# A six-layer perceiver block on one core: when the second batch's values are projected, which PSUM banks hold the last group's turned scores, and how the result is combined and stored

## The chip, the cores and the metric

The kernel runs on one core of one Trainium2 chip. Its engines, as the profile names them, are PE (TensorE, matrix products; PEld is its loading of weights), DVE (VectorE), ACT (ScalarE), POOL (GpSimd) and SP (SyncE, which only issues DMAs here). They have a program each and wait for one another through semaphores. The metric is the device time of one execution in microseconds (us), lower is better. Timed before the change: 976.12 us, the median of three runs (973.57 to 976.53).

## The reference, cut to what matters

Two batches of 256 tokens, 256 channels, pass through six residual layers: cross-attention over a context of 4096 rows per batch (16 heads of 16 channels), a gated convolution block, a quantised feed-forward layer, a second cross-attention, a self-attention, and a mixture of eight experts. The change touches the first and the last.

```
def _L0_xattn_ref(q, k, v, mask, ...):        # first layer, 16 heads, 4096 keys per batch
    q = (layernorm(x) @ Wq.T + bq), k = (ctx @ Wk.T + bk), v = (ctx @ Wv.T + bv)   # by heads of 16
    out = softmax(q @ k.T / 4, masked) @ v
    return out @ Wo.T + bo
...
def _L1_ffn_ref(x, expert_embeddings, first_linear, second_linear):   # last layer
    tokens = x_flat[index].reshape(E, expert_capacity, hidden)        # 64 tokens for each of 8 experts
    inter = jax.nn.relu(jnp.einsum('ech,eih->eci', tokens, first_linear))
    out = jnp.einsum('eci,ehi->ech', inter, second_linear) * vals[:, :, None]
    final = jnp.zeros((n_tokens, hidden), x.dtype).at[index].add(out.reshape(-1, hidden))
x = x + final
```

## The kernel before, in words

**The first cross-attention** takes more than half of the time. A *group* is four heads of one batch; there are eight (numbered 0 to 7 by `gg`, 0 to 3 belong to the first batch). In a group the 4096 keys are taken in 32 *steps* of 128, and the loops go by *pairs* of steps, `m` from 0 to 15. In the order of the PE program, one pair is (with the lines of the profile):

- T, the turned scores (`turned_scores`, L1815): for each step four bf16 matmuls of 256 columns, two to a PSUM bank, so two banks a step. ACT takes the exponential of each bank (`exps`, L756, 128x512), two instructions a step. Below, "exp" is one such instruction.
- S, the row scores of the *next* group (`scores`, L1786): two matmuls of 512 columns, one unit after each step. DVE takes their maximum (`row_tops`, L1119). They run ahead, so that they are all done before the last pairs of group 6; group 7 has none.
- K, a projection of second-batch keys (`project_keys`, L1753), in every second pair of groups 0 and 1.
- C, in pair 1 of a group, the turning of the finished context of the group before (`turn_context`, L1843).
- W, the weighing of values by the exps of the pair *before* (`weigh_values`, L1833): 4 fp32 matmuls of 32 weight columns a step.
- V, a projection of second-batch values (`project_values`, L1763, four fp32 matmuls of 256 columns into one bank), 16 of them, in pairs 1 to 15 of group 3 and pair 0 of group 4. ACT copies the bank to SBUF (`copy_values`, L739).

In the last pair of a group stand also the tops of the next (`turn_max`, L1800, copied by ACT at L747).

The eight PSUM banks are divided so: 0 to 3 hold the row scores S, two units of two banks. Banks 4 to 6 are a ring of three (`RING`) for T, K, V, C and tops, in one order that the function `ring_slots` counts out. `ring_free(slot)` lets PE write slot n only when ACT has drained slot n-3. Bank 7 collects W. PE and ACT both go strictly in their program's order. ACT's order in a pair is: four exps, key copies, in pair 1 the context's copy, in pair 0 the copy of the finished weighing of the group before (`copy_weighed`, L763), then the value copy. In pair 8 of group 7 a small matmul (L1885) sums up the absolute weights of the feed-forward layer, on which the DVE's quantising (L1174 to L1190) and then three weight loads wait.

**The last layer** ends with `combine(q)` (L2473): for each pair q of experts, for each tile i of 128 tokens, one matmul that adds into the PSUM bank i. DVE adds bank i to the residual tile (L1738) once `g_out` says that its q = 3 is done, and SP stores all four tiles with one DMA of 512 KB (L629), when all are added.

Of the kernel before, what the change touches and what calls it, by code (L numbers as in the profile page):

```python
# [11 lines left out]
ALU = mybir.AluOpType  # L12
# [3 lines left out]
P = 128  # L16
# [72 lines left out]


def ring_slots():

    turn = itertools.count()
    keys, values, exps, tops, contexts = {}, {}, {}, {}, {}
    for c in range(ROUNDS):
        for i in range(2):
            if c < NCH:
                keys[0, c, i] = next(turn)
            if c in VALUES_AT:
                values[0, VALUES_AT[c], i] = next(turn)  # L100
    for pair in range(2):
        tops[0, pair] = next(turn)
    for gg in range(GROUPS):
        for m in range(KC // 2):
            if m == KC // 2 - 1 and gg + 1 < GROUPS:
                for pair in range(2):
                    tops[gg + 1, pair] = next(turn)
            for step in (KC * gg + 2 * m, KC * gg + 2 * m + 1):
                for pair in range(2):
                    exps[step, pair] = next(turn)  # L110
            if gg < 2 and m % 2:
                keys[1, 4 * gg + m // 4, m // 2 % 2] = next(turn)
            if gg and m == 1:
                contexts[gg - 1] = next(turn)
            if (gg == 3 and m) or (gg == 4 and m == 0):
                done = KC // 2 * (gg - 3) + m - 1
                values[1, done // 2, done % 2] = next(turn)
    contexts[GROUPS - 1] = next(turn)
    return keys, values, exps, tops, contexts
# [3 lines left out]


def values_after(gg, m):

    if (gg == 3 and m) or (gg == 4 and m == 0):
        return divmod(KC // 2 * (gg - 3) + m - 1, 2)
    return None

# [8 lines left out]
def build(nc, t):  # L139

    ctx = ExitStack()
    with ctx:
# [63 lines left out]
        def ring_heads(slot):  # L206
            return ring_bank(slot).rearrange("p (j n) -> p j n", j=2)

        def unit_banks(n):
# [237 lines left out]
        def _(sp):  # L447
# [179 lines left out]
            load(EMB, by_part("embT"), "const_loaded")  # L627
            sp.wait_ge(on["x_ready"], 6 * TT)
            sp.dma_start(t["out"].rearrange("(t p) c -> p t c", p=P), X).then_inc(out_stored, 16)  # L629
            sp.wait_ge(out_stored, 16)  # L630

# [73 lines left out]
        def _(act):  # L705
# [44 lines left out]
            def exps(step):  # L750
                for pair in range(2):
                    slot = EXP_AT[step, pair]
                    act.wait_ge(ring_filled, slot + 1)
                    if pair == 0 and step >= 4:
                        act.wait_ge(pv_done, step - 3)
                    nc.scalar.activation(PR[step % 4][:, pair * CH:(pair + 1) * CH], ring_bank(slot), ACT.Exp)\  # L756
                      .then_inc(ring_drained, 1)
# [298 lines left out]
        def _(dve):  # L1056
# [113 lines left out]
            def quantise_weights():  # L1170
# [7 lines left out]
                dve.wait_ge(on["w_total"], 1)  # L1178
                mark(nc.vector.tensor_scalar(WMEAN, psum[:, 0, 0:2], 1.0 / (D * FF), 1e-5, ALU.mult, ALU.max))
                done()  # L1180
# [561 lines left out]
        def _(pe):  # L1742
# [61 lines left out]
            def turned_scores(step, masked):  # L1804
# [5 lines left out]
                for pair in range(2):  # L1810
                    slot = EXP_AT[step, pair]
                    ring_free(slot)
                    for u in range(2):
                        j = 2 * pair + u
                        last = nc.tensor.matmul(ring_heads(slot)[:, u, :], KST[gg % 2][0:KROWS, j, kc * P:(kc + 1) * P],  # L1815
                                                QST[0:KROWS, G * g + j, b * S:(b + 1) * S],
                                                start=(u == 0), stop=not masked and u == 1, skip_group_check=True)
                    if masked:
                        for qt in range(2):
                            last = nc.tensor.matmul(ring_heads(slot)[:, :, qt * P:(qt + 1) * P],  # L1820
                                                    MASKB[:, qt, kc * P:(kc + 1) * P],
# [25 lines left out]
            def attend(masked):  # L1847
# [17 lines left out]
                for gg in range(GROUPS):  # L1865
                    for m in range(KC // 2):
# [8 lines left out]
                        if gg and m == 1:  # L1875
                            turn_context(gg - 1)
                        if gg or m:
                            weigh_values(KC * gg + 2 * m - 2)
                            weigh_values(KC * gg + 2 * m - 1)
                        if values_after(gg, m):  # L1880
                            project_values(1, *values_after(gg, m))
                        if gg + 1 == GROUPS and m == KC // 4:
                            pe.wait_ge(on["w_summed"], 2)
                            pe.wait_ge(s_maxed, GROUPS * UNITS)
                            nc.tensor.matmul(psum[:, 0, 0:2], ONES, WSUM, start=True, stop=True)\  # L1885
                              .then_inc(on["w_total"], 1)
# [582 lines left out]

            def combine(q):  # L2470
                pe.wait_ge(on["g_down_copied"], q + 1)
                for i in range(TT):
                    last = nc.tensor.matmul(psum[:, i, 0:256], SELT[:, q, i * P:(i + 1) * P], OE[:, q, :],  # L2473
# [24 lines left out]
            pe.wait_ge(on["g_turned_copied"], 4)  # L2498
            for q in range(4):
                combine(q)  # L2500

# [65 lines left out]
```

## Time and profile before

| | |
|---|---|
| median of three runs | 976.12 us |
| the profiled execution: its own time, its span | 976.69 us, 974.6 us |
| PE, DVE, ACT, POOL busy | 92%, 62%, 49%, 11% of the span |
| TensorE clock granted, mean | 0.968 of full speed |
| groups 0 to 7 of the first cross-attention | about 112 to 539 us of the span |
| in them: second-batch values (V) | 285.7 to 362.8 us |
| in them: group 7 | 499.1 to 539.3 us |
| combine and store | 963.6 us to the end |

The span runs from the first to the last instruction; the execution's own time is 2.1 us longer. "Chain of waits" below is the chain of work that ended last, followed back from the end: each of its pieces released the next. The number behind x counts PE instructions as the hardware has them: an fp32 matmul of the program shows as two.

### The profile page before, as it was taken

To read this page: it belongs to the slowest core of one execution; us is meant where nothing else is said; L and a number is where in the kernel's file an instruction comes from. 1 tells how busy PE (TensorE), PEld (TensorE's weight loads), DVE (VectorE), ACT (ScalarE), POOL (GpSimd) and SP (SyncE) were. 2 spreads that over 40 slices of the span, in tenths; PEclk is the share of its full clock that TensorE was granted. 3 is DMA by queue.
4 is the path that set the end of the run, shared out by engine and by line. 5 is a ranking of instruction groups with operands and counts; after the bars stand their busy time and mean duration, and the time that the engine had idled before them with its cause. 6 is when DMAs were issued, how large, how long until landed. Compare 5 with 4: busy or idle time off the path is not lost.

```text
span 974.6 us, 15294 instructions
## 1 busy us (share of the span) xinstructions
PE 896.3 (92%) x5988; PEld 529.3 (54%) x5988; DVE 608.5 (62%) x1083; ACT 479.8 (49%) x953; POOL 105.7 (11%) x118
## 2 busy tenths in 40 slices
PE   6888999999999999999998898689899999989878
PEld 3445544444555555545544686444784874555635
DVE  5778688778874548888833586847424227379442
ACT  3331557777765557777788432324321210576211
POOL 3320011111000000000000200101000006245100
PEclk9999999999999999999999999869899999999979
DMA  9775634354222011222432600604545640000000
GB/s 312 259 202 199 204 104 141 114 162 138 86 67 76 33 59 56 74 74 74 168 123 79 242 1 1 239 21 152 194 173 208 224 145 29 1 1 1 1 1 22
DMA packets 68836, 108.68 MB, mean 112 GB/s; under 512 B 7062, under 2 KB 42902, under 8 KB 66838
## 3 DMA queue, kind: packets, MB, share of 16 engines
q1 hardware_dynamic: 67100, 101.40, 31.5%
q10 hardware_dynamic: 1664, 6.29, 1.8%
q8 instruction: 49, 0.80, 0.3%
q14 instruction: 23, 0.19, 0.1%
HBM read 93.77 MB, written 13.89 MB: 110 GB/s over the span
## 4 chain that ended last, share of the span: by engine, by line
PE 78%; DVE 6%; ACT 6%; issue 3%; DMA 3%; SPq 2%; POOL 0%; ACTq 0%; DVEq 0%
PE psum L1833 13%; PE psum L1815 11%; PE psum L1786 9%; PE psum L2207 6%; PE psum L2180 5%; PE psum L1969 5%; PE psum L1763 4%; PE psum L2300 4%; PE psum L1753 4%; PE psum L1982 3%; ACT arena L756 3%; DMA kparts<-arena 2%; PE psum L2354 2%; PE psum L2339 1%; PE psum L2372 1%
## 5 line engine op out<-in xcount | busy, mean ns | idle before, releaser
L1119 DVE TENSOR_REDUCE arena<-psum 128x1 f32<-128x1024 f32 x256 | 301.3, 1218 | 109.9 <-PE psum L1786 109.4
L756 ACT ACTIVATE arena<-psum 128x512 f32<-128x512 f32 x512 | 264.6, 603 | 62.1 <-PE psum L1815 61.0
L1815 PE MATMUL psum<-arena 99*128 99x256 bf16 x1024 | 160.2, 274 | 8.9 <-ACT arena L756 4.8
L1786 PE MATMUL psum<-arena 96*128 96x512 bf16 x512 | 152.9, 381 | 8.9 <-DVE arena L1119 4.0
L1815 PEld LDWEIGHTS psum<-arena 99*128 99x128 bf16 x1024 | 79.4, 97 | 107.1 <-ACT arena L756 50.3
L1833 PE MATMUL psum<-arena 128*32 128x256 f32 x2048 | 136.8, 385 | 0.0
L1833 PEld LDWEIGHTS psum<-arena 128*32 128x32 f32 x2048 | 53.5, 109 | 75.4 <-ACT arena L756 36.9
L1753 PE MATMUL psum<-arena 128*128 128x512 f32 x128 | 62.9, 619 | 8.4 <-DMA arena<-ctxT 8.4
L1763 PE MATMUL psum<-arena 128*128 128x256 f32 x256 | 64.7, 389 | 2.1 <-issue 2.1
L1786 PEld LDWEIGHTS psum<-arena 96*128 96x128 bf16 x512 | 49.0, 98 | 28.5 <-DVE arena L1119 11.9
L649 POOL TENSOR_TENSOR arena<-arena 128x512 bf16<-128x512 f32 x34 | 41.4, 1218 | 194.3 <-DVE arena L1105 191.7
L2207 PE MATMUL psum<-arena 128*128 128x256 f32 x256 | 60.0, 390 | 0.0
L1763 PEld LDWEIGHTS psum<-arena 128*128 128x128 f32 x256 | 47.7, 191 | 18.0 <-issue 9.9
L739 ACT ACTIVATE arena<-psum 128x512 f32<-128x512 f32 x32 | 19.1, 597 | 76.4 <-PE psum L1763 76.4
L2180 PE MATMUL psum<-arena 128*128 128x512 f32 x128 | 56.0, 593 | 0.0
L2207 PEld LDWEIGHTS psum<-arena 128*128 128x128 f32 x256 | 49.2, 197 | 6.6
L1969 PE MATMUL psum<-arena 128*128 128x256 f32 x192 | 47.0, 404 | 3.5 <-ACT arena L818 0.9
L1969 PEld LDWEIGHTS psum<-arena 128*128 128x128 f32 x192 | 38.2, 202 | 11.1 <-ACT arena L926 1.3
L733 ACT ACTIVATE arena<-psum,arena 128x512 bf16<-128x512 f32 x32 | 22.0, 687 | 44.2 <-PE psum L1753 40.3
L2300 PE MATMUL psum<-arena 128*128 128x512 f32 x96 | 41.9, 594 | 0.7 <-ACT arena L919 0.7
L1982 PE MATMUL psum<-arena 128*128 128x256 f32 (+1 forms) x160 | 38.1, 399 | 4.2 <-ACT arena L914 2.2
L1753 PEld LDWEIGHTS psum<-arena 128*128 128x128 f32 x128 | 24.5, 200 | 31.5 <-issue 21.4
(244 smaller groups left out, 959.1 us busy)
## 6 DMA issues: line engine op xcount, KB each, us to landing
arena<-kparts SPq DMA_DIRECT2D x192, 128.0 KB, 2.9
kparts<-arena SPq DMA_DIRECT2D x32, 384.0 KB, 3.6
arena<-ctxT SPq DMA_DIRECT2D x20, 512.0 KB, 4.9
arena<-ctx SPq DMA_DIRECT2D x2, 4096.0 KB, 15.1
arena<-mask SPq DMA_DIRECT2D x8, 1024.0 KB, 5.3
arena<-mask ACTq DMA_DIRECT2D x4, 1024.0 KB, 14.5
arena<-ctxT SPq DMA_DIRECT2D x1, 4096.0 KB, 13.9
arena<-ctxT SPq DMA_DIRECT2D x4, 1024.0 KB, 8.2
```

What stands on the lines that cost most here:

```text
L756: nc.scalar.activation(PR[step % 4][:, pair * CH:(pair + 1) * CH], ring_bank(slot), ACT.Exp)\
L1119: nc.vector.tensor_reduce(MX[g % 2][:, col:col + 1], unit_banks(n).rearrange("p b n -> p (b n)"), AX.X, ALU.max).then_inc(s_maxed, 1)
L1753: last = nc.tensor.matmul(ring_bank(slot), WK[:, k, f * P:(f + 1) * P], CTX[n % SLOTS][:, k, :], start=(k == 0), stop=(k == CT - 1))
L1763: last = nc.tensor.matmul(ring_bank(slot)[:, v * 256:(v + 1) * 256], CTX[n % SLOTS][:, k, (2 * i + v) * P:(2 * i + v + 1) * P], WV[:, k, : ...
L1786: last = nc.tensor.matmul(out, q, KST[g % 2][0:ROWS, j, at], start=True, stop=not masked, skip_group_check=True)
L1815: last = nc.tensor.matmul(ring_heads(slot)[:, u, :], KST[gg % 2][0:KROWS, j, kc * P:(kc + 1) * P], QST[0:KROWS, G * g + j, b * S:(b + 1) * S],
L1833: last = nc.tensor.matmul(PV[32 * j:32 * (j + 1), :], V_flat[:, at:at + 32], PR[step % 4][:, j * S:(j + 1) * S], start=(kc == 0), stop=(kc ...
L1969: last = nc.tensor.matmul(out, weights[:, k, m * P:m * P + width], xs[k], start=(k == 0), stop=(k == n - 1))
L1982: last = nc.tensor.matmul(out, lhs[k], weights[:, k, :], start=(k == 0 and not biased), stop=(k == n - 1), skip_group_check=biased)
L2180: last = nc.tensor.matmul(psum[:, unit % 3, :], QC[:, c, w * P:(w + 1) * P], CTXT[w // 2][:, c, n * 512:(n + 1) * 512], start=(c == 0), st ...
L2207: last = nc.tensor.matmul(psum[:, 6, 0:256], PT1[:, k * P:(k + 1) * P], CTXK[w // 2][:, k, :], start=(k == 0), stop=(k == KC - 1), skip_gr ...
L2300: last = nc.tensor.matmul(psum[:, bank, :], HTF[:, c, i * P:(i + 1) * P], WQKV[which][:, c, half * HALF:(half + 1) * HALF], start=(c == 0) ...
```

## The change

1. `values_after` moves the 16 value projections one pair later: pairs 2 to 15 of group 3 and pairs 0 and 1 of group 4. On PE they now stand in front of W of the same pair, not behind it. The order on ACT keeps its form, and the ring is counted out anew.
2. From step `LAST` (the first of group 7) on, the turned scores go to banks 0 to 3 (`exp_bank`: bank 2 (step mod 2) + pair of heads), which S no longer needs. Each then waits for the exp of two steps before on its own bank; it was the exp three slots of the ring before. The sum of the weights goes into a ring bank (`SUM_BANK`) in place of bank 0.
3. `combine` goes by tile: tiles 0 and 1 get q = 0, 1, 2, then both get q = 3, then tiles 2 and 3 get all four each. The store is four DMAs of 128 KB, each issued once its tile is added.

```diff
+def values_after(gg, m):
+
+    if (gg == 3 and m >= 2) or (gg == 4 and m < 2):
+        return divmod(KC // 2 * (gg - 3) + m - 2, 2)
+    return None
...
-    if (gg == 3 and m) or (gg == 4 and m == 0):
-        return divmod(KC // 2 * (gg - 3) + m - 1, 2)
-    return None
+LAST = (GROUPS - 1) * KC
+SUM_BANK = next(4 + i for i in range(RING) if i not in (CONTEXT_AT[GROUPS - 2] % RING, CONTEXT_AT[GROUPS - 1] % RING))
...
+        def exp_bank(step, pair):
+
+            return psum[:, 2 * (step % 2) + pair, :] if step >= LAST else ring_bank(EXP_AT[step, pair])
...
-            sp.wait_ge(on["x_ready"], 6 * TT)
-            sp.dma_start(t["out"].rearrange("(t p) c -> p t c", p=P), X).then_inc(out_stored, 16)
-            sp.wait_ge(out_stored, 16)
+            for i in range(TT):
+                sp.wait_ge(on["x_ready"], 5 * TT + i + 1)
+                sp.dma_start(t["out"][i * P:(i + 1) * P, :], X[:, i, :]).then_inc(out_stored, 16)
+            sp.wait_ge(out_stored, 16 * TT)
...
                 for pair in range(2):
-                    slot = EXP_AT[step, pair]
-                    ring_free(slot)
+                    heads = exp_bank(step, pair).rearrange("p (j n) -> p j n", j=2)
+                    if step < LAST:
+                        ring_free(EXP_AT[step, pair])
+                    elif step < LAST + 2:
+                        pe.wait_ge(s_maxed, GROUPS * UNITS)
+                    else:
+                        pe.wait_ge(ring_drained, EXP_AT[step - 2, pair] + 1)
...
+                        if values_after(gg, m):
+                            project_values(1, *values_after(gg, m))
                         if gg or m:
                             weigh_values(KC * gg + 2 * m - 2)
                             weigh_values(KC * gg + 2 * m - 1)
-                        if values_after(gg, m):
-                            project_values(1, *values_after(gg, m))
                         if gg + 1 == GROUPS and m == KC // 4:
                             pe.wait_ge(on["w_summed"], 2)
-                            pe.wait_ge(s_maxed, GROUPS * UNITS)
-                            nc.tensor.matmul(psum[:, 0, 0:2], ONES, WSUM, start=True, stop=True)\
+                            nc.tensor.matmul(psum[:, SUM_BANK, 0:2], ONES, WSUM, start=True, stop=True)\
...
-            def combine(q):
-                pe.wait_ge(on["g_down_copied"], q + 1)
-                for i in range(TT):
+            def combine(i, *pairs):
+                for q in pairs:
+                    pe.wait_ge(on["g_down_copied"], q + 1)
...
-            for q in range(4):
-                combine(q)
+            combine(0, 0, 1, 2)
+            combine(1, 0, 1, 2)
+            combine(0, 3)
+            combine(1, 3)
+            combine(2, 0, 1, 2, 3)
+            combine(3, 0, 1, 2, 3)
```

PE's program in pairs 1 to 3 of group 3, before (the copy of the program without mask). L1815 is T, L1786 S, L1843 C, L1833 W, L1763 V:

```order
344 L1843 MATMUL psum<-arena 128x128 x2
345 L1833 MATMUL psum<-arena 32x256 x8
346 L1763 MATMUL psum<-arena 128x256 x4
347 L1815 MATMUL psum<-arena 128x256 x4
348 L1786 MATMUL psum<-arena 128x512 x2
349 L1815 MATMUL psum<-arena 128x256 x4
350 L1786 MATMUL psum<-arena 128x512 x2
351 L1833 MATMUL psum<-arena 32x256 x8
352 L1763 MATMUL psum<-arena 128x256 x4
353 L1815 MATMUL psum<-arena 128x256 x4
```

The same place on PE after the change (L1827 is T, L1793 S, L1855 C, L1845 W, L1770 V):

```order
344 L1855 MATMUL psum<-arena 128x128 x2
345 L1845 MATMUL psum<-arena 32x256 x8
346 L1827 MATMUL psum<-arena 128x256 x4
347 L1793 MATMUL psum<-arena 128x512 x2
348 L1827 MATMUL psum<-arena 128x256 x4
349 L1793 MATMUL psum<-arena 128x512 x2
350 L1770 MATMUL psum<-arena 128x256 x4
351 L1845 MATMUL psum<-arena 32x256 x8
352 L1827 MATMUL psum<-arena 128x256 x4
```

V stood between W and the next T; it now stands between S and W. Pair 1 of group 3 has none. In group 7 and in the combine no kind of instruction changes its place on PE; only banks, waits and the operands of the 16 combine matmuls do.

## Rows read from the trace of the kernel before

**Rows 1.** The page, the chain that ended last, shares by engine.

```profile
PE 78%; DVE 6%; ACT 6%; issue 3%; DMA 3%; SPq 2%; POOL 0%; ACTq 0%; DVEq 0%
```

**Rows 2.** Chain of waits, one pair of group 7: start us, us, what.

```profile
508.32 1.00 PE psum L1833 x16
509.32 0.34 PE psum L1815 x2
...
509.68 0.61 ACT arena L756
...
510.33 0.39 PE psum L1815 x2
```

**Rows 3.** Chain of waits, one pair with values, group 3.

```profile
290.67 1.94 PE psum L1763 x8
...
293.12 0.60 ACT arena L756
...
295.60 1.94 PE psum L1763 x8
```

**Rows 4.** Chain of waits, one pair with a key projection, group 1.

```profile
199.66 1.72 PE psum L1753 x4
201.38 1.00 PE psum L1833 x16
202.38 0.54 PE psum L1815 x4
202.92 0.43 PE psum L1786 x2
203.36 0.44 PE psum L1815 x4
```

**Rows 5.** Chain of waits, a value projection near the start.

```profile
29.68 1.73 PE psum L1763 x8
```

**Rows 6.** Chain of waits, group 2's end to pair 1 of group 4.

```profile
274.99 1.00 PE psum L1833 x16
...
278.82 1.00 PE psum L1833 x16
...
284.52 0.22 PE psum L1843 x2
...
285.74 1.94 PE psum L1763 x8
...
365.02 1.00 PE psum L1833 x16
```

**Rows 7.** Timeline of ACT, runs of 128x512 activations.

```profile
509.68 2.06 ACT L756 ACTIVATE arena<-psum 128x512 f32<-128x512 f32 x4 [0.34 <-PE psum L1815]
...
832.57 4.03 ACT L994 ACTIVATE arena<-psum 128x512 f32<-128x512 f32 x8 [23.82 <-PE psum L2311]
```

**Rows 8.** Chain of waits, turning of the context, pair 1 of group 7.

```profile
503.07 0.44 PE psum L1843 x2
```

**Rows 9.** Chain of waits, the last piece.

```profile
970.82 0.42 DVE arena L1738
```

**Rows 10.** Timeline: the last weight load, its first user, the store's issue.

```profile
530.69 1.55 SPq L561 DMA_DIRECT2D arena<-wfuT  x1
...
549.08 1.29 PE L2098 MATMUL psum<-arena 128*32 128x256 f32 x20
...
971.26 0.38 SPq L629 DMA_DIRECT2D out<-arena  x1
```

**Rows 11.** DMA issues: count, KB each, median us from issue to landing.

```profile
arena<-wfuT SPq DMA_DIRECT2D x1, 1024.0 KB, 7.5
...
out<-arena SPq DMA_DIRECT2D x1, 512.0 KB, 2.9
...
arena<-woT SPq DMA_DIRECT2D x1, 256.0 KB, 2.6
```

**Rows 12.** Windows: PE, PEld, DVE, ACT, POOL busy, granted clock, DMA share, GB/s.

```profile
544.00:545.00 1.00, 1.00 (x3) 0.82 (x4) 0.00 (x0) 1.00 (x1) 1.00 (x4) 0.50 1.03 434
```

More of the change, by code:

```diff
@@ L114, in ring_slots @@
                 contexts[gg - 1] = next(turn)
-            if (gg == 3 and m) or (gg == 4 and m == 0):
-                done = KC // 2 * (gg - 3) + m - 1
-                values[1, done // 2, done % 2] = next(turn)
+            if values_after(gg, m):
+                values[(1, *values_after(gg, m))] = next(turn)
     contexts[GROUPS - 1] = next(turn)
@@ L122 @@
 KEY_AT, VALUE_AT, EXP_AT, TOP_AT, CONTEXT_AT = ring_slots()
-def values_after(gg, m):
-    if (gg == 3 and m) or (gg == 4 and m == 0):
-        return divmod(KC // 2 * (gg - 3) + m - 1, 2)
-    return None
+LAST = (GROUPS - 1) * KC
+SUM_BANK = next(4 + i for i in range(RING) if i not in (CONTEXT_AT[GROUPS - 2] % RING, CONTEXT_AT[GROUPS - 1] % RING))
 def keys_at(gg, m):
@@ L755, in exps @@
                         act.wait_ge(pv_done, step - 3)
-                    nc.scalar.activation(PR[step % 4][:, pair * CH:(pair + 1) * CH], ring_bank(slot), ACT.Exp)\
+                    nc.scalar.activation(PR[step % 4][:, pair * CH:(pair + 1) * CH], exp_bank(step, pair), ACT.Exp)\
                       .then_inc(ring_drained, 1)
@@ L1178, in quantise_weights @@
                 dve.wait_ge(on["w_total"], 1)
-                mark(nc.vector.tensor_scalar(WMEAN, psum[:, 0, 0:2], 1.0 / (D * FF), 1e-5, ALU.mult, ALU.max))
+                mark(nc.vector.tensor_scalar(WMEAN, psum[:, SUM_BANK, 0:2], 1.0 / (D * FF), 1e-5, ALU.mult, ALU.max))
                 done()
@@ L1810, in turned_scores @@
                 for pair in range(2):
-                    slot = EXP_AT[step, pair]
-                    ring_free(slot)
+                    heads = exp_bank(step, pair).rearrange("p (j n) -> p j n", j=2)
[5 more added lines that the diff above has]
+                        pe.wait_ge(ring_drained, EXP_AT[step - 2, pair] + 1)
                     for u in range(2):
                         j = 2 * pair + u
-                        last = nc.tensor.matmul(ring_heads(slot)[:, u, :], KST[gg % 2][0:KROWS, j, kc * P:(kc + 1) * P],
+                        last = nc.tensor.matmul(heads[:, u, :], KST[gg % 2][0:KROWS, j, kc * P:(kc + 1) * P],
                                                 QST[0:KROWS, G * g + j, b * S:(b + 1) * S],
@@ L1819, in turned_scores @@
                         for qt in range(2):
-                            last = nc.tensor.matmul(ring_heads(slot)[:, :, qt * P:(qt + 1) * P],
+                            last = nc.tensor.matmul(heads[:, :, qt * P:(qt + 1) * P],
                                                     MASKB[:, qt, kc * P:(kc + 1) * P],
@@ L1876, in attend @@
                             turn_context(gg - 1)
+                        if values_after(gg, m):
+                            project_values(1, *values_after(gg, m))
                         if gg or m:
```

## The prediction

> **What bounds the kernel now.** I read the shares of the chain of waits first, then the chain in order of time at the three places that the change touches, then ACT's timeline there, and the list of DMA issues for the end. PE holds 78% of the chain [rows 1], so time is won where PE waits or where one of its instructions costs more than it must. Where nothing is in the way, a pair of steps is PE's work alone: W 1.00, T 0.54, S 0.43, T 0.44, S 0.43, in all 2.84 us [rows 4]. The first T after W costs 0.54 and the second 0.44: 0.10 us goes for the change from the 32-column weights of W to full ones.
>
> In the pairs with values the chain leaves PE. V ends at 292.61 (290.67 + 1.94), and the next V starts at 295.60 after a W of 1.00, so 1.99 us lie between V and W [rows 3], where T, S, T, S right behind V would take 1.74 (the 1.84 of the row above less the change of 0.10). The reader is to see the exp at 293.12 in the chain: ACT copies V first, only then begins its four exps, and the last T of the pair needs the first exp drained. That is a wait of 0.25 us in each such pair. V itself takes 1.94 us there, but 1.73 near the start, where it does not follow W [rows 5].
>
> In group 7 there is no S between the T's. The chain goes W 1.00, T 0.34, exp 0.61, T 0.39, with 0.07 of signals: 2.41 us [rows 2]. Of these 1.41 lie between two W's. The fourth bank of a pair is the ring's first again, so the fourth T waits for an exp that could only start after the first T. ACT is not full: its four exps fill 2.06 us and then it waits 0.34 [rows 7].
>
> **The values, pairs of groups 3 and 4.** The move takes no instruction away. V goes between S and W. The row that stands nearest to this is the key projection K, which has that place already: 1.72 us, four instructions of 0.43, nothing extra in front of it, then W at its usual 1.00 and T at its usual 0.54 [rows 4]. So I take V at 1.73 and not at 1.94, and no wait behind it: ACT has the 1.00 of W to copy the bank (0.60), before T comes. Its own bank is free in time: V's slot needs the second exp of its pair; that starts about 0.85 us after the pair's first T and ends by 1.5, while V comes at 1.84. The pair is 1.00 + 1.84 + 1.73 = 4.57 against 4.93.
>
> I count from the end of W in pair 1 of group 3 (285.74, where the first V starts) to the end of W in pair 1 of group 4 (366.02): 80.28 us [rows 6], with 16 V in both versions. New: 16 × 2.84 = 45.5, 16 × 1.73 = 27.7, the tops in the last pair 0.98 (3.83 from W to W where no V is in the pair, less 2.85), the context's turning 0.22 [rows 6], together 74.4. One hitch is new: in pair 0 of group 4 the copy of the finished weighing stands ahead of V's copy on ACT, and waits for W, which now ends after V. V's copy comes some 0.3 us after W, so the T's behind it wait, and the next V a little: 0.4 by estimate, from copies of 0.4 and 0.6. Sum 74.8, gain 5.4 us. The ends: if V costs 1.94 wherever it stands, 16 × 0.21 = 3.4 less, so 2.0. Nothing below that but for new waits (last rival). Behind V in the queues: SP's two loads of context chunks wait for value copies that come a pair later; they have about 60 us before their values are projected, and the loads of stacked keys behind them wait for W anyway.
>
> **Group 7, four banks.** Each T now waits for the exp two steps before. PE alone then needs 0.54 + 0.44 = 0.98 between two W's in place of 1.41 [rows 2, 4], a pair of 1.98. Can ACT follow? Eight activations of this shape in a row take 4.03 us, (4.03 - 0.60) / 7 = 0.49 from start to start [rows 7]; four are 1.96, just under 1.98. The last exp of a pair ends at about 0.36 + 3 × 0.49 + 0.60 = 2.43 after the pair's first T began, and the T on its bank comes at 1.98 + 0.66 = 2.64. So PE sets the pace. That gives 0.43 in each of pairs 2 to 15, 14 × 0.43 = 6.0. Pairs 0 and 1 gain only about 0.1 together: C stands in a ring bank still, needs an exp of the same pair drained, and that hangs on ACT, which does the copy of the weighing between; C began at 503.07 [rows 8] and would begin near 502.9. Together 6.1. The final double W meets its exps just in time (2.43 against 2.48). The sum of the weights moves to a bank that has been free since the start of the group, so costs the same.
>
> The ends of this term: if ACT needs the whole 2.06 for each four, with no overlap from one pair to the next, 14 × (2.41 - 2.06) = 4.9. If the wait stays as it is, 0.
>
> The Trainium skill, "ScalarE: Activation LUTs", section "What ACT_TABLE_LOAD costs", gives an activation with immediate operands 186 ns + 0.833 ns a column, with 93 ns of overlap back to back. By that page an exp of 512 columns is 613 ns and 520 from start to start, and four are 2.08 us: ACT would be the bound, and the term would be 14 × 0.33 = 4.6. The trace disagrees by 0.03 us an instruction, and the row with eight in a row decides for me; the rival below has its own number from the row of four.
>
> What follows group 7 comes earlier as a whole. Its last weight load could be late in place of PE: wfuT was issued at 530.69 and takes 7.5 us to land, so about 538.2, and the product that needs it starts at 549.08 [rows 10, 11]. The load hangs on the sum in pair 8, which itself comes 7 × 0.43 = 3 us earlier, while its user comes 6.1 earlier. The slack of 11 us shrinks to 8. Cost nothing.
>
> **Combine and store.** The 16 matmuls stay 16, and the last tile is finished when it was. The last add still starts about 970.82 [rows 9]: it had waited behind three others on DVE, each 0.44, but the last matmul ends just before it too. What is left is the store, 2.9 us for 512 KB [rows 11], issued at 971.26 [rows 10]. The last one carries 128 KB and has no other behind or beside it; tile 2's is some 1.7 us older. The nearest row has 256 KB in 2.6, 0.3 less for half; for a quarter I go on by the same slope to about 2.4, and as that row had two other loads behind it, a bit lower: gain 0.6. The ends: 0, and three quarters of 2.9, 2.2.
>
> **Sum.** 5.4 + 6.1 + 0.6 = 12.1. The profiled execution took 976.69, so 964.6 on its scale. That execution was 0.57 above the median of the runs shown; on the median's scale it is 964.0. I say 964.2.
>
> One thing moves without being touched: stretches at the low clock (1.2 GHz, half speed). PE ran at 0.50 in 544:545 [rows 12], after some tenths of idle time around 543.5, and there are such stretches near 630 to 648, 684 to 691 and 926 to 938. Their length can differ when all comes 12 us earlier; one that is 3 us longer or shorter is 1.5 us of time. This is in the ranges.
>
> **The rivals.**
> (a) ACT becomes the pace of group 7, at 2.06 or a little more for each four exps. For it: 1.96 and 1.98 are nearly equal. Against it: the run of eight. 14 × 0.08 = 1.1 us less gain: 965.3.
> (b) V costs 1.94 in its new place too, because the 0.21 is its own and not W's. For it: all 13 V's of full pairs in group 3 show 1.94. Against it: the 1.73 of rows 5, and K. 3.4 us less: 967.6.
> (c) The change does not do what it says in group 7: the fourth T still waits, because what holds it is not its bank. Against: the chain names the exp, and the pair is exactly the sum of W, T, exp, T. 6.1 less: 970.3.
> (d) Slower than before. V in front of W holds W up: V must find its bank drained by the second exp of its pair. If ACT ran late in these pairs, PE would stand before V, and all of W behind it, where before W came first and covered that. It decides from 0.35 us of lateness (1.84 - 1.5); to come out 3 us above 976.1 the 15 us between must be lost in 16 pairs, 0.94 us each, so ACT would have to be 1.3 us late. ACT has 4 × 0.49 + 0.49 = 2.45 us of work in a pair of 4.57, and before K, with the same need, PE never stood [rows 4]. Time 979 at that lateness.
>
> **How the numbers follow.** Forecast 0.62, its own range 962.2 to 966.5; (a) 0.13, (b) 0.15, (c) 0.06, (d) 0.02; 0.02 for something unseen near no change. The low end is 961.3: the store at its best 1.6 more, and a shorter cold stretch 1.3 more. The high end 968.8 holds (a) and (b), with a cold stretch a little longer, and leaves (c) and (d) out. Faster by over 0.3% (2.9 us, about what a measurement tells from no change): 0.95, as (c) with a gain of 6 is faster too; within 0.3% 0.03; slower 0.02.
>
> **What would show it.** In group 3 V is followed by W and the start of one V to the next is 4.57 us, V 1.73 in the chain, and no exp in it. If V is 1.94, (b). In group 7, W to W is 1.98 and the chain stays on PE; if exps of ACT follow one another in the chain there and W to W is 2.04 or more, (a); if W to W is 2.41, (c). The last store lands in about 2.3 us. I am wrong as a whole if group 3 or 7 is as long as before, or if the gain there is given back behind 540 us, by a load not landed or by more work at half clock.

## The result, and the profile after

The changed kernel takes 965.93 us, the median of four runs (964.62 to 966.81), against 975.52 us for the kernel before beside it (973.57 to 976.53). The ratio is 0.9903 [0.9882, 0.9924]: 9.6 us less. The profiled execution took 966.37 us, with a span of 964.5, 10.1 less than before. The mean granted clock is 0.968 in both.

The shares of the chain, answering to [rows 1]:

```profile
PE 79%; DVE 6%; ACT 5%; DMA 4%; issue 3%; SPq 2%; POOL 0%; ACTq 0%; DVEq 0%
```

The chain of waits in a pair of group 3 with values, answering to [rows 3] (start us, us, what; `...` stands for rows left out; L1770 is V, L1845 W, L1827 T, L1793 S):

```profile
292.26 1.73 PE psum L1770 x8
293.99 1.00 PE psum L1845 x16
294.99 0.54 PE psum L1827 x4
...
296.84 1.73 PE psum L1770 x8
```

V starts every 4.58 us where it was 4.93. V is down from 1.94 to 1.73, and no exp is left between V and the T's.

The same chain in pair 0 of group 4, where the copy of the finished weighing (L770, ahead of V's on ACT) waits for W, and in pair 1, where the context is turned (L1855):

```profile
354.48 1.00 PE psum L1845 x16
355.48 0.34 PE psum L1827 x2
...
355.83 0.25 ACT arena L746
...
356.30 0.61 ACT arena L763
...
357.79 0.22 PE psum L1855 x2
...
358.03 1.96 PE psum L1770 x8
360.00 1.00 PE psum L1845 x16
```

W to W is 5.52 us here. L746, the copy of V's bank, is in the chain: this is the hitch that the prediction had named. The V behind the context's turning takes 1.96, not 1.73.

The chain in group 7, from the W of pair 1 on, answering to [rows 2] (the turning of the context before it, at 503.07 in [rows 8], starts at 497.87 here):

```profile
498.31 1.00 PE psum L1845 x16
499.31 0.98 PE psum L1827 x8
500.29 0.77 PE psum L1845 x9
```

W to W is 1.98 and the four T's stand as one piece of 0.98, where two pieces of T had an exp between them. ACT's and PE's timelines there, answering to [rows 7] (what stands in brackets is the idle time before and what ended it):

```profile
499.67 28.03 ACT L763 ACTIVATE arena<-psum 128x512 f32<-128x512 f32 x56 [0.60 <-PE psum L1827]
```

```profile
526.19 2.21 PE L1845 MATMUL psum<-arena 128*32 128x256 f32 x32
```

ACT runs 56 exps in one row, (28.03 - 0.60) / 55 = 0.499 us from start to start. That includes some 0.24 us in which the first T of pair 9 stood behind the sum of the weights (its exp starts at 513.76, 1.24 after the one two before it, where 0.97 to 1.01 is usual); without them it is just under 0.495, a quarter of the pair's 1.98. From the W of pair 1 up to that sum the chain is PE alone, behind it the chain runs along ACT's exps. The last double W takes 2.21, where the same row took 1.93 before: its last eight instructions start at 527.76, 0.05 after the end of the last exp.

Behind group 7 PE falls to the low clock level, and again later. Windows of after (length in us, then PE, PEld, DVE, ACT, POOL busy, granted clock, DMA share, GB/s), beside [rows 12]:

```profile
531.00:538.00 7.00, 6.31 (x20) 4.83 (x19) 0.67 (x2) 2.48 (x3) 3.21 (x11) 0.51 1.00 421
545.00:548.00 3.00, 3.00 (x7) 2.44 (x8) 2.09 (x7) 0.70 (x2) 0.00 (x0) 0.50 0.04 14
616.00:643.00 27.00, 18.39 (x67) 12.73 (x68) 15.35 (x44) 6.53 (x11) 0.00 (x0) 0.51 0.36 132
```

0.50 is 1.2 GHz. Before, there was one such stretch here, from 543.5 to 546.9; now there are two, from 531.2 to 538.0 and from 544.8 to 548.2. The same piece of work in the chains of before and of after shows what the second one costs:

```profile
554.50 20.99 PE psum L1969 x96
```

```profile
545.00 22.57 PE psum L1980 x96
```

The end, answering to [rows 9, 11], the last add and the stores (count, KB each, median us from issue to landing):

```profile
961.99 0.42 DVE arena L1745
```

```profile
out<-arena SPq DMA_DIRECT2D x4, 128.0 KB, 1.7
```

Where the 10.1 us of span came from: the stretch of values (end of W in pair 1 of group 3 to the same in group 4, 285.84 to 361.00) is 75.16 instead of 80.28, 5.1 less. Group 7 (494.13 to 528.44) is 34.31 instead of 40.18, 5.9 less. From the last add's end to the end of the span it is 2.1 instead of 3.4, 1.3 less. Together 12.3. The lead over before is 10.9 us at the end of group 7 (528.44 against 539.34): 11.0 from the two places, less 0.1 because the first began 0.1 later. At the start of the last add it is 8.8 (961.99 against 970.82). So 2.1 us were given back between.

### The profile page after: what moved, and what is told of

It reads as the page before. It is cut to its first block, busy times and chain, and to the rows that moved or that the text cites. A ratio compares the mean times of both kernels' runs of the same rounds, so it can differ in the third digit from the quotient of the medians.

```text
span 964.5 us, 15296 instructions
## 1 busy us (share of the span) xinstructions
PE 889.4 (92%) x5988; PEld 530.3 (55%) x5988; DVE 608.8 (63%) x1083; ACT 480.1 (50%) x953; POOL 105.6 (11%) x118
## 4 chain that ended last, share of the span: by engine, by line
PE 79%; DVE 6%; ACT 5%; DMA 4%; issue 3%; SPq 2%; POOL 0%; ACTq 0%; DVEq 0%
PE psum L1845 12%; PE psum L1827 11%; PE psum L1793 10%; PE psum L2218 6%; PE psum L2191 6%; PE psum L1980 5%; PE psum L2311 4%; PE psum L1770 4%; PE psum L1760 4%; PE psum L1993 3%; ACT arena L763 2%; DMA kparts<-arena 2%; PE psum L2365 2%; PE psum L2350 1%; PE psum L2383 1%
## 5 line engine op out<-in xcount | busy, mean ns | idle before, releaser
L1793 PE MATMUL psum<-arena 96*128 96x512 bf16 x512 | 152.9, 381 | 11.0 <-DMA arena<-kparts 5.9
L1827 PE MATMUL psum<-arena 99*128 99x256 bf16 x1024 | 155.1, 274 | 3.5 <-ACT arena L754 1.2
L1845 PE MATMUL psum<-arena 128*32 128x256 f32 x2048 | 137.0, 385 | 0.1
L1827 PEld LDWEIGHTS psum<-arena 99*128 99x128 bf16 x1024 | 80.6, 97 | 98.2 <-ACT arena L763 36.7
L1845 PEld LDWEIGHTS psum<-arena 128*32 128x32 f32 x2048 | 53.4, 109 | 74.6 <-ACT arena L763 31.1
L1793 PEld LDWEIGHTS psum<-arena 96*128 96x128 bf16 x512 | 48.8, 98 | 30.6 <-DVE arena L1126 13.0
L1770 PE MATMUL psum<-arena 128*128 128x256 f32 x256 | 63.2, 383 | 2.1 <-issue 2.0
L1770 PEld LDWEIGHTS psum<-arena 128*128 128x128 f32 x256 | 48.1, 192 | 15.0 <-issue 6.9
L1980 PE MATMUL psum<-arena 128*128 128x256 f32 x192 | 48.6, 413 | 3.5 <-ACT arena L825 0.9
L746 ACT ACTIVATE arena<-psum 128x512 f32<-128x512 f32 x32 | 19.1, 598 | 58.0 <-PE psum L1770 58.0
L1980 PEld LDWEIGHTS psum<-arena 128*128 128x128 f32 x192 | 39.3, 208 | 11.6 <-ACT arena L933 1.3
L740 ACT ACTIVATE arena<-psum,arena 128x512 bf16<-128x512 f32 x32 | 22.0, 687 | 43.5 <-PE psum L1760 39.4
L1993 PE MATMUL psum<-arena 128*128 128x256 f32 (+1 forms) x160 | 38.5, 401 | 4.2 <-ACT arena L921 2.2
```

Of the source, the lines that this page charges most:

```text
L1770: last = nc.tensor.matmul(ring_bank(slot)[:, v * 256:(v + 1) * 256], CTX[n % SLOTS][:, k, (2 * i + v) * P:(2 * i + v + 1) * P], WV[:, k, : ...
L1793: last = nc.tensor.matmul(out, q, KST[g % 2][0:ROWS, j, at], start=True, stop=not masked, skip_group_check=True)
L1827: last = nc.tensor.matmul(heads[:, u, :], KST[gg % 2][0:KROWS, j, kc * P:(kc + 1) * P], QST[0:KROWS, G * g + j, b * S:(b + 1) * S], start= ...
L1845: last = nc.tensor.matmul(PV[32 * j:32 * (j + 1), :], V_flat[:, at:at + 32], PR[step % 4][:, j * S:(j + 1) * S], start=(kc == 0), stop=(kc ...
L1980: last = nc.tensor.matmul(out, weights[:, k, m * P:m * P + width], xs[k], start=(k == 0), stop=(k == n - 1))
L1993: last = nc.tensor.matmul(out, lhs[k], weights[:, k, :], start=(k == 0 and not biased), stop=(k == n - 1), skip_group_check=biased)
```

## The experiments

Each is built on one of the two kernels. Kernels measured in one session share the runs of before, so the time of before differs a little from case to case (976.8 to 977.2).

**Values alone.** Part 1 of the change on the kernel before (the new `values_after` with it):

```diff
...
+                        if values_after(gg, m):
+                            project_values(1, *values_after(gg, m))
                         if gg or m:
                             weigh_values(KC * gg + 2 * m - 2)
                             weigh_values(KC * gg + 2 * m - 1)
-                        if values_after(gg, m):
-                            project_values(1, *values_after(gg, m))
```

> Part 1 alone: values one pair later and in front of the weighing. Theory: V 1.73 us in its new place, from one V to the next 4.57, groups 3 and 4 shorter by 5.1 us as in the changed kernel; time 975.5 - 5.1 = 970.4, give or take 1.5 for low-clock stretches. Rival (the gain needs the other parts, or V costs 1.94 when alone): 973.5.

972.42 us (8 runs) against 977.02, ratio 0.9946 [0.9924, 0.9968]: 5.3 us less by the ratio, 4.6 by the medians. The median is 0.5 above the range that I expected. The place itself is as expected: V at 1.73, V to V 4.58, and the stretch of values is 75.16 us (287.69 to 362.85), as in the changed kernel. Behind group 7 this execution has a long stretch at the low clock, which comes up again below.

**Late, but still behind W.** The same slots one pair later, V left in its old place:

```diff
-    if (gg == 3 and m) or (gg == 4 and m == 0):
-        return divmod(KC // 2 * (gg - 3) + m - 1, 2)
+    if (gg == 3 and m >= 2) or (gg == 4 and m < 2):
+        return divmod(KC // 2 * (gg - 3) + m - 2, 2)
```

> Values one pair later, but still behind the weighing (half of part 1). Theory: it is the place and not the lateness that counts, so V still 1.94 us, the wait of 0.25 still there, 4.93 from V to V, and 975.5, no change. Rival: the lateness alone gives part of the 5.1, time 971 to 974.

976.76 us (12 runs) against 977.02, ratio 0.9979 [0.9958, 1.0000]. The chain:

```profile
292.47 1.94 PE psum L1764 x8
...
294.44 0.02 ACT arena L740
...
294.93 0.60 ACT arena L757
...
296.40 1.00 PE psum L1834 x16
297.40 1.94 PE psum L1764 x8
```

V is 1.94, V to V is 4.93 and the exp is in the chain, all as before. From the end of W in pair 1 of group 3 to the end of W in pair 2 of group 4 it is 83.13 us (284.70 to 367.83), a plain pair of 2.85 more than the 80.28 of before. The gain hangs on the place in front of W. The delay of a pair gives nothing in the chain; for the whole kernel the interval reaches from no change to 4.1 us less.

**Keys behind the weighing.** The converse, on the changed kernel: K goes to the place that V had (the ring and ACT's order follow, which the diff leaves out).

```diff
-                        if keys_at(gg, m):
-                            project_keys(1, *keys_at(gg, m))
                         if gg and m == 1:
                             turn_context(gg - 1)
...
                             weigh_values(KC * gg + 2 * m - 1)
+                        if keys_at(gg, m):
+                            project_keys(1, *keys_at(gg, m))
```

> The changed kernel with the 16 key projections of groups 0 and 1 moved from in front of the weighing to behind it (the place that values had before). Theory (an fp32 product with 128 weight columns costs 0.21 us more right behind the 32-column weighing, and ACT's copy then stands before the exps): K 1.93 us in place of 1.72, a wait of 0.2 to 0.3 (more, as ACT makes two copies of 0.6), from one K to the next (two pairs) 7.9 to 8.4 in place of 7.41; 8 to 15 us more in all, about 977. Rival (the 0.21 was the value projection's own): K stays 1.72.

983.09 us in one execution, span 981.3, 16.7 more than the changed kernel's profiled one. K to K (two pairs):

```profile
195.83 1.93 PE psum L1760 x4
...
197.78 0.03 ACT arena L740
...
198.37 0.68 ACT arena L741
199.05 0.50 ACT arena L763
...
203.26 1.00 PE psum L1845 x16
204.26 1.93 PE psum L1760 x4
```

K rises from 1.72 to 1.93, by the same 0.21 as V, though it is other work. So the 0.21 belongs to the place behind W and not to V. The rows of PEld show where it sits, here V behind W in before, behind S in after, and behind the turning of the context in after:

```profile
290.60 1.59 PEld L1763 LDWEIGHTS psum<-arena 128*128 128x128 f32 x8 [0.41 <-issue]
```

```profile
287.40 1.61 PEld L1770 LDWEIGHTS psum<-arena 128*128 128x128 f32 x8 [0.21 <-issue]
```

```profile
358.00 1.59 PEld L1770 LDWEIGHTS psum<-arena 128*128 128x128 f32 x8 [0.23 <-issue]
```

By the chain these three V's begin at 290.67, 287.69 and 358.03. A load of these weights takes 0.19. Behind S the first one starts 0.29 before V and is done when V begins; behind W it starts 0.07 before and behind the context's turning 0.03 before, and V is 0.21 and 0.23 longer. The weights of the turning are 128 columns wide like V's own. So the change from 32 columns to 128 can't be the whole reason for a late first load. Behind W it may be; behind the turning, whose two products take 0.22 in all, V's bank is also freed by the third exp of the pair, which ends at 357.89. No run separates these.

The period is 8.43 instead of twice 2.84 plus 1.73, 7.41. The wait is larger than V's: ACT makes two copies of K (L740, L741) before its first exp. Period and time came out above what I had expected, the time by 6 us.

**Four banks alone.** Part 2 on the kernel before (`exp_bank`, `LAST` and `SUM_BANK` as in the change's diff, the values and the end as before).

> Part 2 alone: group 7 in four banks. Theory: 1.98 us from W to W in group 7, 5.9 us less up to the end of the last W. After it the changed kernel ran 6.9 us at the low clock where before had 3.5. If that comes from how group 7 now runs, this kernel shows the long stretch right behind the last W too, and 971.0 to 971.5; if it is only where the stretch falls, 969.6 give or take 1.5.

971.14 us (6 runs), ratio 0.9938 [0.9915, 0.9962]: 6.1 us less by the ratio, 5.9 by the medians. The chain, W to W 1.98:

```profile
504.33 0.98 PE psum L1826 x8
505.31 1.00 PE psum L1844 x16
```

It has the long stretch at the low clock behind group 7 (534.0 to 540.8), and the time is the one that I had expected with it. The conclusion that I had tied to this, that the stretch comes from how group 7 runs, does not hold: see the part on why the prediction was right.

**Combine and store alone.** Part 3 on the kernel before.

> Part 3 alone: combine by tile, four stores. Theory: from the last add to the end 2.1 us in place of 3.4, all else as before: 974.2. Rival (the stores cost issue time or the order of the combine matmuls costs PE time): 975.5 or more.

976.37 us (12 runs), ratio 0.9999 [0.9985, 1.0014]. Its last add ends at 971.57 and the span at 973.7, so the end is 2.1 us as it is after the change, while the total can't show 1.3; the 974.2 that I expected did not come. The interval reaches from 1.5 us less to 1.4 more, so for the time of the whole kernel this part stays inconclusive.

**Half of the weighing, and a quarter.** In group 7 two of the four heads (then three of four) are not weighed after the first step. If the four 32-column products of W ran one behind another, W would shrink and show what paces the pair.

```diff
-                for j in range(G):
+                for j in range(2 if gg == GROUPS - 1 and kc else G):
```

> The changed kernel with heads 2 and 3 of group 7 left out of the weighing from the second step on (that part of the result is missing), so PE has 0.5 us less in each pair there and ACT sets the pace. Measures ACT alone. Theory: 4 exps in 1.95 to 1.98, so W to W 1.96 and hardly any gain (0.3 us in 14 pairs): PE and ACT are within 2% of one another in the four-bank form. Rival (a): 2.06, longer than now. Rival (PE alone paced it and ACT has room): 1.5 to 1.8.

> The changed kernel with heads 1 to 3 of group 7 left out of the weighing from the second step on (that part of the result is missing). With two heads left W took 0.99 us, as with four, so nothing was learned of ACT; with one it should be 0.5. PE alone would then make a pair in 1.48. Theory: ACT paces at 4 x 0.487 to 0.493 = 1.95 to 1.97. Rival (a, by the Trainium skill's 520 ns an exp): 2.08 is already excluded by 1.98 now; if the pair falls clearly below 1.95, ACT had more room than I said.

965.87 us with two heads, 962.18 with one, in one execution each. The chains of the two:

```profile
506.46 0.99 PE psum L1845 x8
```

```profile
503.52 0.98 PE psum L1827 x8
504.50 0.98 PE psum L1845 x4
```

W stays at 0.98 to 1.00 with 16, 8 or 4 instructions. So both experiments failed at what they were for: PE wasn't freed. They showed instead that the four 32-column products of a step run side by side and cost what one costs. That ACT stretches W is unlikely: in pair 1, right behind a wait for ACT, a W of 10 instructions takes 0.98 too (496.66 in the kernel with one head). ACT's timeline in the kernel with one head:

```profile
502.41 8.92 ACT L763 ACTIVATE arena<-psum 128x512 f32<-128x512 f32 x18
```

(8.92 - 0.60) / 17 = 0.489 us from start to start. Four are 1.96, as the pair is (504.50 to 506.46), and as PE's own 0.98 + 0.98. PE and ACT are within 0.02 of each other, and no run here tells which holds the other.

**Four banks two pairs earlier.** In the last two pairs of group 6 the row scores are done as well:

```diff
-LAST = (GROUPS - 1) * KC
+LAST = (GROUPS - 1) * KC - 4
...
-                ring_free(slot)
+                if gg < GROUPS - 2:
+                    ring_free(slot)
```

> The changed kernel with the four banks from the last two pairs of group 6 on (their row scores are done), and the turning of group 6's and 7's contexts without the wait for the ring, whose bank is long free. Theory: 0.43 in each of these two pairs (a little less in the last, with the tops), and the turning in pair 1 of group 7, now at 497.87, about 1.0 earlier: 1.7 us up to the end of the last W; time 964.2 give or take 1.5. Rival (the first T in bank 0 waits for the last maxima, or ACT's copy of the weighing holds the turning anyway): 965.9.

961.77 us (6 runs) against 977.16, ratio 0.9853 [0.9817, 0.9889]. The last W ends at 527.32 instead of 528.44, though the stretch began 0.3 us later: 1.4 gained. Near the hand-over to group 7 the chain reads:

```profile
495.71 0.98 PE psum L1827 x8
496.69 0.30 PE psum L1856 x2
496.99 1.00 PE psum L1845 x16
```

The turning of the context costs 0.30 in its place, with no exp before it. The median is 0.9 below the range that I expected, 4.2 below the changed kernel's, of which the banks explain 1.4. In the profiled executions the stretches at the low clock behind group 7 are 3 us shorter in all (55 against 58).

**Keeping PE busy behind group 7.** To see what the low clock gives back: the changed kernel with ten more bf16 products of 512 columns, whose result nobody uses, in PE's waits between 527 and 545 us.

```diff
+            def keep_busy(bank, count):
+                for _ in range(count):
+                    nc.tensor.matmul(psum[:, bank, :].rearrange("p (j n) -> p j n", j=4), IDENTB,
+                                     IDENTB.unsqueeze(1).broadcast_to((P, 4, P)), start=True, stop=True,
+                                     skip_group_check=True)
...
                 weigh_values(GROUPS * KC - 1)
+                keep_busy(0, 2)
                 turn_context(GROUPS - 1)
```

> The changed kernel with 10 bf16 products of 512 columns, whose results nobody reads, put on PE where it waits between the end of group 7 and the convolution block (2 before the last turning, 2 and then 3 + 3 before and behind the two turnings of x). Theory (the 2.1 us that the changed kernel gives back behind 528 us are stretches at the low clock after short idle times): no low clock from 528 to 550, 2 to 3 us less, 963.4. Rival (the clock falls for another reason, or the products delay PE): low clock as before, 966 to 968.

962.71 us (6 runs) against 976.76, ratio 0.9873 [0.9843, 0.9904]. The median is 3.2 below the changed kernel's, as expected, but the two intervals overlap and the six runs reach from 957.72 to 966.46, so the size is uncertain. The window and chain of its profiled execution (957.72 us, the lowest of the six):

```profile
527.00:550.00 23.00, 22.20 (x134) 15.95 (x126) 15.89 (x49) 10.48 (x21) 5.57 (x20) 1.00 0.68 260
```

```profile
531.97 3.73 PE psum L2000 x16
```

The clock stays at 1.00 for the whole window, and the projection that took 5.72 us in after (L1993 there, under 0.51) takes 3.73.

**Keeping PE busy in all such places.** The same, with more products before and between the quantised layer's turnings (22, 4, 2, 4, 10), in the second cross-attention, and around the router.

> As warm_end, with such products also in PE's other long waits: the quantised layer (22, 4, 2, 4, 10, 2, 1), before the fourth turning of exps (14), before the last projection of the second attention (2), around the router (8, 2, 17, 5). Theory: the stretches at half clock at 616 to 644, 678 to 682, 788 to 791 and 916 to 927 go, and the products behind them take half: about 6 + 1 + 1 + 2.5 us on top of warm_end, 953 to 956. Rival (the waits are on DVE anyway and little PE work in them is on the chain, or the extra products run late): 962 to 967.

950.40 us (6 runs) against 976.76, ratio 0.9746 [0.9714, 0.9778], 2.6 below the range that I expected. Windows over the places that were slow (a low stretch of some 4 us is left at 609 to 613, and one at 531 to 535):

```profile
610.00:635.00 25.00, 23.28 (x117) 12.86 (x116) 17.74 (x50) 6.53 (x11) 1.50 (x1) 0.94 0.47 169
896.00:912.00 16.00, 14.43 (x86) 9.02 (x84) 7.70 (x35) 2.89 (x5) 0.00 (x0) 1.00 0.00 0
```

**The kernel before, kept busy too.** The same products in the kernel without the change. If the low clock took back part of the gain, the difference between this kernel and the last one is larger than the 10.1 us of the plain pair.

> The kernel before with the same extra products in PE's waits as warm_all. It leaves the low clock out of both sides, so the difference to warm_all (950.4) is the change itself. Theory (5.1 + 5.9 + 1.3 = 12.3 are saved at the places of the change, and what was given back was low clock): 962 to 963.5. Rival (the 2.1 are given back by something that the change does): 960.

964.42 us (6 runs) against 977.16, ratio 0.9867 [0.9829, 0.9906]: 14.0 above the kernel with the change, by medians, and 0.9 above the range that I expected. The spans of the two profiled executions are 963.1 and 947.7, 15.4 apart. 2.6 us of this are not the change's: they differ by 2.62 us already at the end of W in pair 1 of group 3 (287.48 against 284.86). From there to the end of the last W it is 253.57 us and 242.54, 11.0 less, the same as between the plain kernels. Then the difference dips to 12.4 at the end of the projection (549.46 against 537.03), over the changed kernel's low stretch at 531 to 535, and goes to 14.1 over one of the other at 579 to 583 (its projection L2009 takes 5.38, the changed kernel's L2020 3.69). From there it stays: 14.1 to 14.2 at 587, 603, 738, 897 and 934 us of the changed one, and the store adds its 1.3. Without the 2.6 this is 12.8, against 12.3 at the three places. With the clock high nearly throughout, nothing is given back in the end.

**Both together.** Four banks two pairs earlier and all the products, with 12 of them ahead of the wait for the hidden rows of the quantised layer and 14 behind it.

> early_banks and warm_all together, with the extra products of the quantised layer spread: 12 ahead of the wait for the hidden layer, 14 (not 22) behind it, since in warm_all PE stood idle for 2.70 us there, the clock fell, and 22 products at half clock ran into the time of the turning. Theory: 1.7 less from the banks, 1 to 3 less from the quantised layer: 946.5. Rival (the clock falls there all the same, the products delay the turning): 948.7.

949.06 us (6 runs, 944.50 to 952.37) against 977.16, ratio 0.9720 [0.9681, 0.9758]. This is the rival that I had named at 948.7, not the 946.5. The median is the lowest of all, but only 1.3 under that of the kernel without the earlier banks, and the intervals overlap, so the two can't be told apart. The products themselves come too many at one place:

```profile
608.93 2.70 issue
611.63 5.78 PE psum L1753 x26
617.42 0.46 PE psum L2074 x8
```

L1753 are the extra products. PE begins them only after 2.70 us at the end of the `If` that holds the cross-attention and the convolution block, in which no engine is waited for. From the end of the projection to the turning it is 8.5 us, where the kernel without them needs 6.3. By estimate (0.22 us a product, 5.78 / 26) 16 products in place of 26 would win some 2 us more; that wasn't tried.

## Why the prediction was right, and where its terms were off

The forecast was 964.2, in a range of its own of 962.2 to 966.5; measured were 965.93.

**V at 1.73 and no wait behind it: right.** The chain shows both, and the move of K shows that the 0.21 belongs to the place behind W. That it is the price of going from 32-column weights to full ones, as the prediction has it, is shown only in part: the same extra stands behind the turning of the context, where no widths change. Rival (b) (V at 1.94 in the new place) is out. So is (d): PE never stands before V in group 3.

**The hitch between groups 3 and 4: mechanism right, size too small.** I had 0.4 for it; the chain shows 5.52 - 4.57 - 0.22 = 0.7. Two things make it: the wait for L746, as foreseen, and a V of 1.96 behind the turning of the context, which I had priced at 1.73. There V's bank hangs on the third exp of the pair, since the turning takes a place of the ring too, and not on the second as I had written for all pairs. The term of the values came out at 5.1 instead of 5.4.

**Group 7 at 1.98 from W to W: right.** ACT takes 0.489 to 0.495 for an exp of 512 columns in a row of 18 to 56. Rival (c), a fourth bank that does nothing, is out. The 2.06 of rival (a) is out as well, and with it the 520 ns that follow from the Trainium skill, "ScalarE: Activation LUTs", section "What ACT_TABLE_LOAD costs". But my sentence that PE sets the pace is not shown: the two are a tie, and behind pair 8 the chain goes along ACT. The term came out at 5.9 instead of 6.1, because "just in time" for the final double W was late: 2.21 where it took 1.93 before.

**The store: too small.** I had 0.6, by the slope from 512 to 256 KB. The measured landing is 1.7 us for 128 KB, and the end is 1.3 us shorter.

**Sum of the three places: 12.3 for a predicted 12.1.** That it is so near is luck: 0.3 and 0.2 too much at the first two, 0.7 too little at the store. What came out at the end of the span was 10.1, and this is the term that I had only put into the range: the stretches at the low clock. The lead goes from 10.9 at 528.44 to 10.1 at the projection (533.93 against 543.98), to 9.5 at the start of the 96 products of L1980 (545.00 against 554.50), and to 7.9 at their end (567.57 against 575.49). All three losses stand where the changed kernel is at the low clock. It then swings between 7.6 and 9.6 with each slow stretch, to 8.8. Counted over windows of 1 us, both profiled executions spend some 61 us at the low level, but before has 7 of them ahead of the groups and 55 behind group 7, the changed kernel 3 and 58. With PE kept busy in both kernels nothing is lost in the end, so I count it as shown that the give-back belongs to the clock.

Why the stretches fall as they do stays open. The changed kernel falls to the low level 2.7 us behind its last W and for 6.8 us, where before fell 4.2 us behind it and for 3.4. It would be natural to blame the denser group 7, and the kernel with four banks alone has the long stretch too. But so have two kernels whose group 7 is that of before. The windows of values alone and of late, but still behind W:

```profile
541.00:547.00 6.00, 6.00 (x15) 4.74 (x16) 1.85 (x5) 1.05 (x1) 0.91 (x4) 0.50 1.00 422
```

```profile
541.00:547.00 6.00, 5.31 (x16) 4.09 (x16) 0.42 (x1) 2.48 (x3) 3.06 (x11) 0.50 1.01 423
```

Both are low for 6.8 us (540.2 to 547.0 and 540.9 to 547.7), and the kernel with one head, whose group 7 is dense, only for 3.4 (530.5 to 533.9). So the long stretch does not need the change. The 2.1 is the value of this pair of executions, and how near the total came to the forecast is in part luck as well.

What made the forecast hold was that the large terms were differences between rows of the same trace in the same form of work (K's place for V's, the row of eight exps). The small ones, estimated from neighbours of another size, were off by 0.3 to 0.7 us, in both directions.

## What to carry to other kernels

Look in the trace for the same instruction at two durations. The difference can come from what stands in front of it, and the rows of the weight loads show whether it does; a swap of two independent pieces can take it away together with a wait. Before pricing another buffer, compare the two engines' work in the period it leaves: here it ended in a tie, so by this count a fifth bank has nothing to win (not tried). And where a kernel falls to the low clock after short waits, a gain of microseconds may be partly given back; filling PE's waits there was worth more than the whole change, by medians (12.7 us against 9.6). Before blaming the change for a slow stretch, look whether kernels without it have the same one.

## What the runs showed of the hardware

- Behind the 32-column products of W, the next products with 128 weight columns cost PE 0.21 us more with fp32 weights (V 1.94 against 1.73, K 1.93 against 1.72) and 0.10 with bf16 ones (T 0.54 against 0.44). Their first weights are loaded when W is nearly over (0.07 us before V begins, where it is 0.29 behind S). Behind the two short full-width products of the context's turning V costs 1.96, with its first load 0.03 us before it.
- One, two or four 32-column products at different positions cost the same: 0.98, 0.99 and 1.00 us for a pair of steps with 4, 8 and 16 instructions.
- PE fell to 1.2 GHz after or within short waits: in the changed kernel at 531.2, after a wait of 0.55 us at 528.44, in the kernel before at 543.5, 0.7 us into a wait. Ten extra products in such waits kept it at 2.4 GHz from 527 to 550. In all such places such products were worth 12.7 us in the kernel before (977.16 to 964.42) and 15.5 in the changed one (965.93 to 950.40, with before at 975.52 and 976.76 beside them).
- 128 KB stores landed in 1.7 us, the one of 512 KB in 2.9.
- PE spends 2.70 us at the end of the branch ahead of the quantised layer's second half, where no wait for an engine shows (in each of two kernels with extra products right behind it).
- Runs of one kernel differ by up to 1% (before: 968.91 to 979.60 in one session); the mean granted clock of these two is 0.973 and 0.965.
